# Mixture-of-experts stage of a two-layer gated cross-attention kernel: from chunks of 256 rows to chunks of 640

## What is computed

```python
        B, S, D = hidden_states.shape          # 8, 512, 256
        E = wg.shape[1]                        # 8
        N = B * S
        k = TOP_K                              # 2
        C = k * int(CAP_FACTOR * ((N + E - 1) // E))      # 1280
...
        disp = buf[:E * C].reshape(E, C, D)
        h = jax.nn.silu(jnp.einsum('ecd,ehd->ech', disp, fc1_w) + fc1_b[:, None, :])   # 1024 wide
        y = jnp.einsum('ech,ehd->ecd', h, fc2_w) + fc2_b[:, None, :]
        ybuf = jnp.concatenate([y.reshape(E * C, D), jnp.zeros((1, D), y.dtype)], 0)
        combined = jnp.sum(gates[..., None] * ybuf[pos], axis=1)
```

## Time and profile before

| | us |
|---|---|
| median of 3 runs (1765.41 to 1767.84) | 1765.98 |
| profiled execution: its own time | 1756.83 |
| profiled execution: span from first to last instruction | 1754.8 |
| stretch from the first L1573 to the last L1592 of `experts` | 505.7 |

### The profile page before, as it was taken

The page is one execution under the profiler, slowest core; times in us unless marked ns, Lnnn a source line. Parts: engine busy times, 40 slices in busy tenths (PEclk is TensorE's granted clock), DMA queues, the critical chain, the costliest instruction groups (busy, mean ns, idle before and its releaser), DMA issues. The chain is left out here.

```text
span 1754.8 us, 30445 instructions
## 1 busy us (share of the span) xinstructions
PE 1543.1 (88%) x11934; PEld 1024.4 (58%) x11934; DVE 1267.6 (72%) x1964; ACT 979.2 (56%) x1339; POOL 634.1 (36%) x957
## 2 busy tenths in 40 slices
PE   6868999999978269999999999868959999999855
PEld 5753333333357268999999999834523333333444
DVE  5649999999744856654555554368769999999687
ACT  4534888888823033444454535335527888888544
POOL 3203555555212134433332333243214444553020
PEclk9986999999988579999999999979969999999986
DMA  7653455555362112133222311057644554554102
GB/s 243 240 215 102 125 126 123 120 119 120 76 241 87 54 61 85 45 95 96 73 65 90 97 40 49 31 175 246 217 117 102 120 124 120 119 125 109 41 1 97
DMA packets 117278, 198.71 MB, mean 113 GB/s; under 512 B 28480, under 2 KB 62080, under 8 KB 116112
## 3 DMA queue, kind: packets, MB, share of 16 engines
q1 hardware_dynamic: 83632, 112.30, 20.2%
q0 software_dynamic: 33504, 84.47, 19.2%
HBM read 117.77 MB, written 77.87 MB: 111 GB/s over the span
## 5 line engine op out<-in xcount | busy, mean ns | idle before, releaser
L1000 DVE TENSOR_REDUCE a_nmax<-a_ring 128x2 f32<-128x1024 f32 x512 | 608.8, 1219 | 41.8 <-PE a_ring L916 41.5
L987 ACT ACTIVATE i_room<-a_ring 128x1024 f32<-128x1024 f32 x512 | 522.5, 1026 | 155.1 <-PE a_ring L926 155.1
L938 PE MATMUL a_pout<-i_room,values 128*17 128x256 f32 x4096 | 322.1, 387 | 0.7 <-ACT i_room L987 0.7
L1613 ACT ACTIVATE e_full<-e_pH,b1T 128x256 f32<-128x256 f32 x320 | 133.6, 468 | 272.0 <-PE e_pH L1573 269.9
L1642 DVE TENSOR_TENSOR e_hid_lo<-e_full,e_hid_hi 128x512 fp32r<-128x512 f32 x160 | 128.3, 805 | 159.0 <-ACT e_hid_hi L1621 157.5
L1592 PE MATMUL e_pY<-fc_w_hi,e_hid_hi 128*128 128x256 f32 x640 | 186.0, 291 | 9.8 <-DVE e_hid_lo L1642 9.8
L1682 POOL DMA_INDIRECT ytok<-w,slot_put x80 | 78.9, 986 | 302.4 <-DVE w L1657 290.2
L1573 PE MATMUL e_pH<-e_rowsT_hi,fc_w1T_hi 128*128 128x256 f32 x640 | 182.1, 284 | 1.5 <-DVE e_rowsT_lo L1488 1.5
L1573 PE MATMUL e_pH<-e_rowsT_lo,fc_w1T_hi 128*128 128x256 f32 x640 | 181.8, 284 | 0.0
L1573 PE MATMUL e_pH<-e_rowsT_hi,fc_w1T_lo 128*128 128x256 f32 x640 | 181.8, 284 | 0.0
L1592 PE MATMUL e_pY<-fc_w_hi,e_hid_lo 128*128 128x256 f32 x640 | 181.0, 283 | 0.0
(11 more groups left out here) (307 smaller groups left out, 2602.7 us busy)
## 6 DMA issues: line engine op xcount, KB each, us to landing
ks<-i_room SPq DMA_DIRECT2D x64, 256.0 KB
qs<-i_room SPq DMA_DIRECT2D x64, 256.0 KB
outs<-a_osb SPq DMA_DIRECT2D x64, 256.0 KB, 2.6
fc_raw<-in_L_ffn_fc_w SPq DMA_DIRECT2D x16, 1024.0 KB, 5.5
BIG<-outs SPq DMA_DIRECT2D x64, 128.0 KB
ytok<-r_zeros SPq DMA_DIRECT2D x8, 1024.0 KB, 9.8
c_yg<-ytok POOLq DMA_DIRECT2D x16, 512.0 KB, 6.5
i_k<-ks POOLq DMA_DIRECT2D x56, 128.0 KB, 3.3
```

Of the source, the lines that this page charges most:

```text
L938: mm = e.matmul(pout[n % 2][32 * h:32 * h + VW, at], v[:, b * TPB + t, g * HG + h, :], pexp[t][:, h, at], start=(t == 0 and half == 0), st ...
L987: e.activation(pexp[t][:, 2 * p:2 * p + 2, :], score_bank(n * U + i)[:, :, :], ACT.Exp).then_inc(exped, 1)
L1000: e.tensor_reduce(nmax[n % 2][:, :].rearrange("p (x y t) -> p x y t", x=2, y=2)[:, :, p, t], max_bank(m)[:, :, :], AX.X, ALU.max, negate=T ...
L1613: ins = e.activation(full[q % 2][:, f % 2, :], pH[q][:, f % 2, :], ACT.Silu, bias=S.b1T[:, ds(n * KF + f, 1)])
```

## The change

The chunks become 640 rows (five tiles), two for each expert, 16 in all. What follows from it and what goes with it:

- First product: a slice of 128 hidden values now takes two halves of 320 rows, 6 matmuls of 320 columns each, into one PSUM bank for each half (`pH[0]`, `pH[1]`).
- Second product: it is no longer done after all eight slices but slice by slice, two slices behind the first product (`SKEW`), into five banks `pY[0]` to `pY[4]`, one for each tile of rows. The high and low part of `w2` lie side by side for each slice, so that one matmul moves both (512 columns) past `hid` high, and one of 256 columns moves `w2` high past `hid` low into the first half of the bank. The two halves of the bank are added by VectorE (`take_output`), two additions for each tile.
- `hid` is now a ring of three slices. All transposes (rows and weights) share one bank, `turned`: four groups for the weights in steps 0, 2, 3, 4 of an expert's first chunk, three groups for the next chunk's rows in steps 5, 6, 7 of every chunk. The second weight is cut in the expert's second chunk.
- One buffer `fc_raw` serves both weights; expert 0's first weight has one of its own inside `place`. One buffer each for gathered rows and for results.
- In `place` one group of transposes stands ahead of each quarter's sum, and ScalarE rounds one part of each weight in turn.
- The loops are written out over steps; POOL's additions stay.

```diff
-CHUNK = 256
+CHUNK = 5 * P
 NCH = CAP // CHUNK
+TILES = CHUNK // P
+WIDE = CHUNK // 2
 VW = DH + 1
...
+        S.fc.first_raw(sb("raw_first", [P, KF, D]))
...
-                for w in range(S.fc.GROUPS):
-                    S.fc.turn_fc1(e, 0, 0, w)
                 for qq in range(QUARTERS):
+                    S.fc.turn_fc1(e, 0, 0, qq)
                     e.wait_ge(built, qq + 1)
...
-                S.fc.load_fc2(e, 1)
...
-                for w in range(S.fc.GROUPS):
                     S.fc.cut_fc2_high(e, 0, 0, w)
...
-        self.raw1, self.raw2 = sb("raw1", [P, KF, D]), sb("raw2", [P, KF, D])
+        self.raw = sb("raw", [P, KF, D])
...
-        self.w2 = [parts(f"w2{x}", [P, KF, D]) for x in range(2)]
-        self.pw = [self.ctx.enter_context(S.nc.psum_tensor(f"fc_pw{j}", [P, 4, P], F32)) for j in range(2)]
+        self.w2 = [sb(f"w2{x}", [P, KF, 2, D], F32R) for x in range(2)]
+        self.turned = self.ctx.enter_context(S.nc.psum_tensor("fc_turned", [P, 4, P], F32))
...
     def load_fc1(self, e, n):
-        if past(n * self.GROUPS):
-            e.wait_ge(self.trw, n * self.GROUPS)
-        e.dma_start(self.raw1[:, :, :], self.S.a["L0_ffn_fc1_w"][ds(n, 1), :, :].rearrange("o (j p) d -> p (o j) d", p=P)
+        if n:
+            e.wait_ge(self.w2e, n * 2 * self.GROUPS)
+        e.dma_start(self.raw_fc1(n)[:, :, :], self.S.a["L0_ffn_fc1_w"][ds(n, 1), :, :].rearrange("o (j p) d -> p (o j) d", p=P)
...
+        if n:
+            e.wait_ge(self.trw, (n + 1) * self.GROUPS)
+        e.dma_start(self.raw[:, :, :], self.S.a["L0_ffn_fc2_w"][ds(n, 1), :, :].rearrange("o (j p) d -> p (o j) d", p=P)
...
-        if past((m - 1) * 2):
-            e.wait_ge(self.wte, (m - 1) * 2)
+        if m:
+            e.wait_ge(self.wte, m * 2)
...
-        full = [sb(f"full{q}", [P, 2, CHUNK]) for q in range(2)]
-        hid = parts("hid", [P, KF, CHUNK])
...
-        rows = [S.w["wq0"], S.w["wk0"]]
-        y = [S.w["wv0"], S.w["wo0"]]
-        pX = ps("pX", [P, KD, CHUNK])
-        pH = [ps(f"pH{j}", [P, 2, CHUNK]) for j in range(KF // 2)]
-        pY = ps("pY", [P, 2, D])
...
+        full = [sb(f"full{q}", [P, CHUNK]) for q in range(2)]
+        hid = [parts(f"hid{j}", [P, CHUNK]) for j in range(3)]
+        y = sb("y", [P, TILES, D])
+        rows = S.w0[:, :, :, :].rearrange("p a k d -> p (a k) d")[:, 0:TILES, :]
+        pH = [ps(f"pH{j}", [P, SEQ]) for j in range(2)]
+        pY = [ps(f"pY{t}", [P, 2, D]) for t in range(TILES)]
...
+        CHUNKS, STEPS = E * NCH, E * NCH * KF
+        ROW_GROUPS = (0, 2), (2, 4), (4, 5)
+        WEIGHT_STEPS, ROW_STEPS = (0, 2, 3, 4), (5, 6, 7)
+        SKEW = 2
...
+                e.dma_start(b2[:, :], a["L0_ffn_fc2_b"][0:1, :].broadcast_to([P, D])).then_inc(ldb, 16)
+                for n in range(1, E):
+                    fc.load_fc2(e, n)
+                    if n + 1 < E:
+                        fc.load_fc1(e, n + 1)
+                    e.wait_ge(ye, n * NCH * TILES)
+                    e.dma_start(b2[:, :], a["L0_ffn_fc2_b"][n:n + 1, :].broadcast_to([P, D])).then_inc(ldb, 16)
...
+                def turn_rows(m, g):
+                    t0, t1 = ROW_GROUPS[g]
+                    if g < 2:
+                        e.wait_ge(ldr[g], 16 * (2 if g == 0 else 3) * (m + 1))
+                    if m or g:
+                        e.wait_ge(rte, 6 * m + 2 * g)
                     for k in range(KD):
-                        for t in range(2):
-                            last = e.transpose(pX[:, k, t * P:(t + 1) * P], rows[j][:, t, k * P:(k + 1) * P], S.ident[:, :])
+                        for t in range(t0, t1):
+                            last = e.transpose(turned[:, 2 * k + t - t0, :], rows[:, t, k * P:(k + 1) * P], S.ident[:, :])
                     last.then_inc(trr, 1)
...
+                def hidden(s):
+                    m, f = s // KF, s % KF
+                    x, j = m // NCH % 2, m % 2
+                    if f == 0 and m % NCH == 0:
+                        e.wait_ge(fc.wte, (m // NCH + 1) * WG * 2)
+                    for h in range(2):
+                        if f == 0:
+                            e.wait_ge(rte, 6 * m + 4 + 2 * h)
+                        if s:
+                            e.wait_ge(act, 2 * s - 1 + h)
+                        for k in range(KD):
+                            for n_pass, (pl, pr) in enumerate(PASSES):
+                                mm = e.matmul(pH[h][:, 0:WIDE], w1T[x][pl][:, k, f * P:(f + 1) * P],
+                                              rowsT[j][pr][:, k, h * WIDE:(h + 1) * WIDE],
+                                              start=(k == 0 and n_pass == 0), stop=(k == KD - 1 and n_pass == 2))
+                        mm.then_inc(up, 1)
+
+                def output(s):
+                    m, f = s // KF, s % KF
+                    x = m // NCH % 2
+                    if f == 0 and m % NCH == 0:
+                        e.wait_ge(fc.w2e, (m // NCH + 1) * WG * 2)
+                    e.wait_ge(lo, s + 1)
+                    for t in range(TILES):
+                        if f == 0 and m:
+                            e.wait_ge(ye, (m - 1) * TILES + t + 1)
+                        token = slice(t * P, (t + 1) * P)
+                        e.matmul(pY[t][:, :, :], hid[s % 3][HI][:, token], w2[x][:, f, :, :], start=(f == 0), stop=False)
+                        mm = e.matmul(pY[t][:, HI, :], hid[s % 3][LO][:, token], w2[x][:, f, HI, :],
+                                      start=False, stop=(f == KF - 1))
+                        if f == KF - 1:
                             mm.then_inc(down, 1)
...
+                    if f < KF - 1:
+                        mm.then_inc(used, 1)
...
+                for s in range(STEPS + SKEW):
+                    m, f = s // KF, s % KF
+                    n = m // NCH
+                    if s < STEPS:
+                        hidden(s)
+                        if f in WEIGHT_STEPS and m % NCH == 0 and n + 1 < E:
+                            fc.turn_fc1(e, n + 1, (n + 1) % 2, WEIGHT_STEPS.index(f))
+                        if f in ROW_STEPS and m + 1 < CHUNKS:
+                            if f == ROW_STEPS[0] and m % NCH == 0 and n + 1 < E:
+                                e.wait_ge(fc.wte, 2 * WG * (n + 2))
+                            turn_rows(m + 1, ROW_STEPS.index(f))
+                    if s >= SKEW:
+                        output(s - SKEW)
...
+                for s in range(STEPS):
+                    m, f = s // KF, s % KF
+                    n = m // NCH
+                    if s >= 2:
+                        e.wait_ge(lo, s - 1)
+                    for h in range(2):
+                        e.wait_ge(up, 2 * s + h + 1)
+                        e.activation(full[s % 2][:, h * WIDE:(h + 1) * WIDE], pH[h][:, 0:WIDE], ACT.Silu,
+                                     bias=S.b1T[:, n * KF + f:n * KF + f + 1]).then_inc(act, 1)
+                    if s >= 3:
+                        done = s - 3
+                        if done % KF == KF - 1:
+                            e.wait_ge(down, (done // KF + 1) * TILES)
+                        else:
+                            e.wait_ge(used, done // KF * (KF - 1) + done % KF + 1)
+                    e.wait_ge(act, 2 * s + 2)
+                    e.activation(hid[s % 3][HI][:, :], full[s % 2][:, :], ACT.Copy).then_inc(hi, 1)
...
+                def take_rows(m, g):
+                    t0, t1 = ROW_GROUPS[g]
+                    e.wait_ge(trr, 3 * m + g + 1)
+                    src = turned[:, :, :].rearrange("p (k t) q -> p k t q", k=KD)[:, :, 0:t1 - t0, :]
+                    part = lambda p: by_tile(rowsT[m % 2][p][:, :, t0 * P:t1 * P])
+                    cut(e, part(HI), part(LO), src, rte, 6 * m + 2 * g)
+
+                def take_output(m):
+                    def first(t):
+                        e.wait_ge(down, m * TILES + t + 1)
+                        e.tensor_tensor(y[:, t, :], pY[t][:, LO, :], b2[:, :], ALU.add).then_inc(summed, 1)
+
+                    e.wait_ge(ldb, 16 * (m // NCH + 1))
+                    if m:
+                        e.wait_ge(yst, 16 * TILES * m)
+                    first(0)
+                    for t in range(TILES):
+                        if t + 1 < TILES:
+                            first(t + 1)
+                        e.wait_ge(summed, m * TILES + t + 1)
+                        e.tensor_tensor(y[:, t, :], pY[t][:, HI, :], y[:, t, :], ALU.add).then_inc(ye, 1)
...
+                    n = m // NCH
+                    if s < STEPS:
+                        if f in WEIGHT_STEPS and n + 1 < E:
+                            w = WEIGHT_STEPS.index(f)
+                            if m % NCH == 0:
+                                fc.take_fc1(e, n + 1, (n + 1) % 2, w)
+                            else:
+                                fc.cut_fc2(e, n + 1, (n + 1) % 2, w)
+                        if f in ROW_STEPS and m + 1 < CHUNKS:
```

(21 more changed lines are left out.)

178 lines of the change are left out of this document (30 added, 148 removed).

## The result

The kernel after takes 1734.82 us (median of 4 runs, 1732.07 to 1736.94); the kernel before, run beside it, 1765.70 us. The ratio is 0.984, 95% interval 0.982 to 0.985. The direction was right and the size was not. The profiled execution of after took 1736.94 us, with a span of 1734.9 us, 19.9 us less than the span of the profiled execution of before. So profile and median already disagree on the size (20 or 31 us), and that is the first thing to explain.

A forecast was written before the change was run, and what follows sets the result against it. TensorE's own work was taken to bound `experts`; -4.4 (matmuls) - 10.4 (waits) + 4.2 - 3.3 (start) + 3.3 (end) = -10.6 us, so 1765.98 becomes 1755.4 us, range 1739 to 1766.

The forecast's parts named there:

- The profile and the median: Whole kernel: the median of before lies 9.15 us above its profiled execution, added unchanged to the forecast for after.
- part 2: TensorE's waits in `experts`: needing a slice's product two slices later cuts waits and restarts from 13.4 to 3, -10.4 us.
- Part 1: Matmuls in `experts`: fewer, wider ones at pitches 0.149, 0.2355 and 0.120 us bring 460.8 to 456.4, -4.4 us.
- The second rival: Matmuls in `experts`: the pitch's excess is per matmul, giving -13.6 us or more, 1746 us; chance 0.18.
- The transposes: TensorE in `experts`: 272 transposes at a pitch of 0.11, 29.9 us; no gain or loss booked for them.
- the cover: Low `hid` in `experts`: ready 1.8 us before it is needed, plus whatever the transposes add, hiding POOL's additions.
- The 2 us at the ends of chunks: Joins of two chunks in `experts`: VectorE's ten additions free banks 0.1 to 0.2 us late; 2 us booked.
- the 1 us for the bank `turned`: Transposes in `experts`: small delays as groups sharing one bank wait for each other's cuts; 1 us booked.
- Part 3: `place` and start of `experts`: waiting for four gathered tiles costs +4.2 us; the reordered sum in `place` saves 3.3 us.
- Part 4: End of `experts`: five last scatters end 6.5 us behind TensorE instead of 3.2, +3.3 us.
- The ends of chunks: Joins of chunks: VectorE additions at 0.69 us make TensorE 2.5 us late 15 times, +37 us, 1791; chance 0.07.
- The clock: TensorE in `experts`: short waits at the joins let its clock fall 15 times, +24 us, 1779; chance 0.02.

The follow-up runs named there:

- before again: The kernel before, unchanged, run again for another trace: 1763.43 us in the first follow-up set, 1764.87 us in a later one.
- after again: The kernel after, unchanged, run again: 1734.15 us in the first follow-up set, 1736.87 and 1737.11 us in later ones.

## Why the prediction was wrong, point by point

Two steps failed, and the mechanisms held. The difference between profile and median was carried over as if it had nothing to do with the change; it hid some 7 us of waits, so that the waits were booked at 10.4 us where some 21 went. And the pitches were booked at 4.4 us where 8.4 went.

The stage is best compared between two kernels of one set: before again (512.8 us from first to last matmul, with TensorE's waits at 16.3 us) and after again (481.2 us), -31.6 us, where the forecast had -14.8 for pitches and waits. Summed over the starts of TensorE's instructions, some 21 us of it are waits with their restarts, 8.4 the pitches, and 0.6 less time at the low clock; what is left is under 2 us.

- **The profile and the median.** This step failed, and it cost most. I took the 9.15 us between the profiled execution and the median of before as equal on both sides. They are not: some 7 us of them are waits of the second kind, in the stage (505.7 us in the first profile, 512.2 and 512.8 in the two later ones on chips where before takes near 1764 us), and the change removes them as well; the same 7 us stand in part 2 below. After has no such gap: its profiled execution is 2 us above its median.
- **Part 1, the matmuls.** Forecast -4.4 us with 0.149, 0.2355 and 0.120. Measured 0.147, 0.236 and 0.118 (medians), which give 1536 x 0.147 + 640 x 0.354 = 452.4 instead of 460.8: -8.4 us. The mechanism held, the size was too small by half; the 320-column pitch is the one of a fixed excess, and 256 columns cost a little less beside 512. The second rival, excess per matmul, holds for 320 columns but not for 512, where it asked for 0.227. By the formula that the Trainium skill gives for the gap of an isolated matmul ("TensorE: Matmul & The Clock Gate", Back-to-back issue gap) 320 columns take 0.136 us (an estimate from it) and 512 take 0.216; the trace disagrees at both, by 0.011 and 0.020 us.
- **The transposes.** Booked at nothing, and nearly right. Their own starts add up to 3.4 us less in after, which looks like a gain. But the last of a group hands 0.08 us on to the matmul behind it (0.03 us until the next start, then 0.31 instead of 0.235), after has 73 such ends in the stage and before 39, and so 2.7 of the 3.4 us come back in the matmuls; 0.6 are six transposes more ahead of the stage.
- **Part 2, the waits.** Forecast 13.4 down to 3. The sign, the place and the cover were right (the doubled additions cost nothing, the lag of one slice 35 us), but both ends were off: the waits with their restarts were some 21 us where before takes near 1764 us, and they went to nothing. The cause that I named, GpSimd's additions, makes nearly all of the 9.8 us in the first profile (seven waits, 8.8 us), but only about half of the waits there (8.5 of 16.1 us stay without the additions). I had seen "ten places" in the earlier trace rows and looked at the long ones only. The 2 us at the ends of chunks and the 1 us for the bank `turned` didn't come.
- **Part 3, the start.** The first gather comes 3.4 us nearer to the start of `place` than before (53.9 us after it instead of 57.3), and from the first gather to the first matmul it takes 11.0 us instead of 6.9, +4.1 us. Forecast were -3.3 and +4.2. The -3.3 came out by luck, as two misses that cancel: the order alone brings the gather 5.1 us nearer, and the other changes in `place`, taken as 0, cost 1.7. In after three of VectorE's one-hot tiles take 1.3 us instead of 0.25, each beside one of GpSimd's cuts of weights. The first matmul came at 632.34 us, 0.8 us later by this count; the rest of the 1.7 us is what lies ahead of `place`, later by that much in this execution.
- **Part 4, the end.** The last scatter ends at 1119.67 us, 6.15 us behind the last matmul (1113.52), where it was 3.2: +2.9 us, forecast +3.3. Right.
- **The rivals.** None of them came. The ends of chunks (+37 us, 0.07; by its own sum 1792 us and not 1791) did not wait at all with a lag of two: VectorE's additions of 256 elements take 0.41 us in after and start 0.33 us apart, where 0.45 was assumed. With a lag of one they did. The clock (+24 us, 0.02) is 1.00 in the stage of after, with seven banks in turn, so the clock that swings as a kernel goes round the PSUM banks, of which the Trainium skill tells ("TensorE: Matmul & The Clock Gate", A second HAM failure mode: psum-queue depth-cycling), isn't borne out here; the page ties it to small idle times between groups of matmuls, and after has next to none.

So of the 16.8 us that the stage gained beyond the forecast, some 11 are waits and their restarts, 4.0 the pitches, and the rest the clock and the transposes. The start and the end, +3.7 us together where +4.2 were forecast, came out right, the start in part by luck.

## What to carry to other kernels

A wait list with a total and a longest hides kinds: look at the start of each wait against the place in the loop, and ask of every place, also the short ones, what lies between the two products there. And before a profile's sum is set against a median, take the gap between the two as time of some stage; it goes where that stage is rewritten, and one profiled execution can be the lucky one. A second product that follows the first by one slice more costs a third buffer for `hid`, and here it covered both a named disturbance, GpSimd's additions, and one that nobody has explained, TensorE's late signal. It does not cost a longer end: with a lag of one slice the last scatter also ends 6.2 us behind the last matmul, so the 2.9 us come with the five tiles of a chunk. And where an instruction waits for several semaphores, the one that the profile names is only the last to change: look whether the instruction needs that change at all.

## What the runs showed of the hardware

- A matmul's signal can come late: in 11 or 12 chunks of 40 on some chips, and in none to two on others, the semaphore update of the last matmul before a group of transposes stands 0.9 to 1.1 us behind the end that the profile gives for the matmul, while TensorE works on; elsewhere it stands 0.01 to 0.4 us behind. The silu that waits for it starts 0.02 us after it, also in the midst of a subtraction on VectorE (694.08 us against 693.37 to 696.20).
- A matmul of these types costs 0.110 us at 128 columns, 0.118 to 0.120 at 256, 0.147 at 320 and 0.231 to 0.236 at 512, from start to start.
- Behind two of six idle times of 2.1 us TensorE's granted clock fell to the lower level (0.53 over the next 3.4 us), behind the other four it was 1.00; behind idle times up to 1.4 us in before it was 1.00.
- The last of a group of transposes takes 0.03 us until the next matmul starts, and the matmul behind it 0.08 us more than usual; the two cancel.
